# A causal depthwise convolution as matmuls: tap matrices stored channel by channel, and the preceding tokens copied by GpSimd

## The reference

```
def _causal_dwconv(x, w):
    k = w.shape[-1]
    xp = jnp.pad(x, ((0, 0), (k - 1, 0), (0, 0))).transpose(0, 2, 1)
    y = jax.lax.conv_general_dilated(xp, w[:, None, :], (1,), 'VALID', feature_group_count=w.shape[0], ...)
    return y.transpose(0, 2, 1)
...
local_short = fir(vh, fir_short_w)      # 5 taps a channel
local_long = fir(vh, fir_long_w)        # 64 taps a channel
```

## Time and profile before

| | |
|---|---|
| time of three runs | 6015.63, 6020.67, 6024.58 us; median 6020.67 |
| the profiled execution | 6031.09 us, its span 6029.3 us |
| the convolution, first to last matmul of L1155 | about 2734 to 3043 us of the span |
| busy over the whole span | PE 5421.1, PEld 4326.3, DVE 4262.5, ACT 2668.0, POOL 2549.7 us |
| mean granted clock of TensorE | 0.926 of 2.4 GHz |

### The profile page before, as it was taken

The page is one execution under the profiler, slowest core; times in us unless marked ns, Lnnn a source line. Parts: engine busy times, 40 slices in busy tenths (PEclk is TensorE's granted clock), DMA queues, the critical chain, the costliest instruction groups (busy, mean ns, idle before and its releaser), DMA issues. The chain is left out here.

```text
span 6029.3 us, 119845 instructions
## 1 busy us (share of the span) xinstructions
PE 5421.1 (90%) x42776; PEld 4326.3 (72%) x42776; DVE 4262.5 (71%) x13841; ACT 2668.0 (44%) x6214; POOL 2549.7 (42%) x3716
## 2 busy tenths in 40 slices
PE   6999999999999999979966645999999999999987
PEld 5888888888888888859954433777777777777765
DVE  4777777777777777752127885888887888888861
ACT  2555555555555555531133321444444444444441
POOL 1222222222222222210057751666666666666660
PEclk9999999999999999989965555999999999999998
DMA  1011101101110110118855542222222222222211
GB/s 41 29 34 36 33 31 36 36 29 34 36 36 29 34 36 29 34 39 186 201 140 147 141 111 63 61 62 61 61 61 61 61 61 62 61 62 61 61 35 44
DMA packets 603925, 373.22 MB, mean 62 GB/s; under 512 B 336528, under 2 KB 589264, under 8 KB 603344
## 3 DMA queue, kind: packets, MB, share of 16 engines
q1 hardware_dynamic: 532880, 329.91, 19.9%
q10 hardware_dynamic: 65664, 16.78, 1.2%
q0 software_dynamic: 4800, 18.88, 1.0%
HBM read 212.59 MB, written 137.10 MB: 58 GB/s over the span
## 5 line engine op out<-in xcount | busy, mean ns | idle before, releaser
L526 POOL TENSOR_TENSOR a_shift<-a_mean_var,a_eps 128x2 f32<-128x2 f32 x256 | 71.3, 278 | 1833.5 <-DVE a_mean_var L736 1833.5
L2125 PE MATMUL c_bank<-c_xT,c_gate 128*128 128x512 f32 x1024 | 499.8, 611 | 1.9 <-ACT c_statsT L1878 1.9
L750 DVE SCALAR_TENSOR_TENSOR a_cv<-a_raw,a_taps,a_cv 128x256 f32<-128x256 f32 x1152 | 461.9, 479 | 19.5 <-ACT a_cv L628 10.0
L820 PE MATMUL a_bank<-a_w,a_hidden 128*128 128x256 f32 x2048 | 459.1, 382 | 0.9 <-ACT a_hidden L613 0.9
L918 PE MATMUL a_bank<-a_turned,a_w 128*128 128x256 f32 x2048 | 453.0, 379 | 1.1 <-ACT a_turned L574 1.1
L820 PEld LDWEIGHTS a_bank<-a_w,a_hidden 128*128 128x128 f32 x2048 | 383.8, 190 | 71.8 <-issue 20.6
L918 PEld LDWEIGHTS a_bank<-a_turned,a_w 128*128 128x128 f32 x2048 | 384.0, 190 | 51.2 <-ACT a_turned L574 1.6
L1775 POOL TENSOR_TENSOR c_expd<-c_e,c_logit 128x16 f32<-128x16 f32 x128 | 371.7, 2904 | 51.1 <-DVE c_logit L1961 38.7
L1761 POOL TENSOR_TENSOR c_stats<-c_l2sq,half 128x16 f32<-128x16 f32 x128 | 373.4, 2917 | 17.8 <-DVE c_l2sq L1950 17.8
L2129 PEld LDWEIGHTS c_bank<-c_statsT,c_gate_stats 128*128 128x128 f32 x2048 | 270.1, 192 | 123.8 <-issue 123.8
L1345 POOL TENSOR_TENSOR i_coef<-i_base,i_exponent 128x12 f32<-128x12 f32 x128 | 298.6, 2332 | 76.7 <-issue 53.5
(11 more groups left out here) (294 smaller groups left out, 14194.1 us busy)
## 6 DMA issues: line engine op xcount, KB each, us to landing
a_x<-in_x SPq DMA_DIRECT2D x64, 256.0 KB, 3.3
scratch_xb<-a_xb SPq DMA_DIRECT2D x64, 256.0 KB, 2.1
scratch_q<-a_qkv_rows SPq DMA_DIRECT2D x64, 256.0 KB, 2.2
scratch_k<-a_qkv_rows SPq DMA_DIRECT2D x64, 256.0 KB, 2.7
scratch_v<-a_qkv_rows SPq DMA_DIRECT2D x64, 256.0 KB, 3.0
b_window<-scratch_v SPq DMA_DIRECT2D x8, 2048.0 KB, 22.2
scratch_long<-b_out ACTq DMA_DIRECT2D x8, 2048.0 KB, 24.6
scratch_short<-b_out POOLq DMA_DIRECT2D x8, 2048.0 KB, 18.4
```

Source lines behind the costliest of these rows:

```text
L750: ins = dve.scalar_tensor_tensor(cv[s][:, n, c], raw[s][:, n, c, j:j + TOK], taps[:, n, c, j:j + 1], cv[s][:, n, c], ALU.mult, ALU.add)
L820: ins = pe.matmul(dst[:, t * D:(t + 1) * D], src[s][:, c, tile_cols(t)], weight[:, c], start=(c == 0), stop=(c == chunks - 1))
L2125: pe.matmul(dst[:].rearrange("p (h t) -> p h t", h=H), gate1[:, c, cols], xT[sl][:, c:c + 1].broadcast_to([P, H, P]), start=(c == 0), stop ...
```

## The change

1. `matrix` becomes `[P, CH, K2, HALF]`: the 128 columns of a channel's matrix lie next to each other. The copies that fill it write in another order, and the matmul reads `matrix[g % 2][:, c]`. The windows keep their layout.
2. SP issues only loads. The copy of the preceding 64 tokens is made by GpSimd: 8 `tensor_copy`, one a sequence, each of 15 blocks of 64 elements on 64 partitions. It waits for the load of its unit. On GpSimd's list the shifts of units 0 and 1 come first, and that of unit u + 2 behind the short store of unit u.
3. TensorE waits for GpSimd's semaphore, which counts one a unit, instead of for the transfer's.

```diff
-        matrix = [sb(f"matrix{g}", [P, K2, HALF, CH]) for g in range(2)]
+        matrix = [sb(f"matrix{g}", [P, CH, K2, HALF]) for g in range(2)]
...
                 sp.dma_start(window[h][HALF:P], v_v[g, h]).then_inc(v_in[h], 16)
-                sp.wait_ge(v_in[h], 16 * (g + 1))
-                now, prev = (window[h][rows].rearrange("p (b n) c -> p b n c", b=SEQS)
-                             for rows in (slice(HALF, P), slice(0, HALF)))
-                sp.dma_start(prev[:, :, 1:WINDOWS], now[:, :, 0:WINDOWS - 1]).then_inc(window_in[h], 16)
...
+            def shift(u):
+
+                g, h = UNITS[u]
+                now, prev = (window[h][rows].rearrange("p (b n) c -> p b n c", b=SEQS)
+                             for rows in (slice(HALF, P), slice(0, HALF)))
+                pool.wait_ge(v_in[h], 16 * (g + 1))
+                for b in range(SEQS):
+                    ins = pool.tensor_copy(prev[:, b, 1:WINDOWS], now[:, b, 0:WINDOWS - 1])
+                ins.then_inc(window_in[h], 1)
+
+            for u in range(PARTS):
+                shift(u)
             for u, (g, h) in enumerate(UNITS):
                 for e in ("act", "dve"):
                     pool.wait_ge(out_made[e], counted(e, "out", u))
                 pool.dma_start(out_v["short"][g, h], out_sb[h][HALF:P]).then_inc(stored["short"][h], 16)
+                if u + PARTS < len(UNITS):
+                    shift(u + PARTS)
...
-                    ins = copy(matrix[g % 2][:, :, m * COLUMNS:(m + 1) * COLUMNS],
-                               src[:].rearrange("p (i k c) -> p k i c", k=K2, c=CH))
+                    ins = copy(matrix[g % 2][:, :, :, m * COLUMNS:(m + 1) * COLUMNS],
+                               src[:].rearrange("p (i k c) -> p c k i", k=K2, c=CH))
...
-                        pe.wait_ge(window_in[h], 16 * (g + 1))
+                        pe.wait_ge(window_in[h], g + 1)
...
-                        taps_of = matrix[g % 2][:].rearrange("p k i c -> p (k i) c")[:, :, c]
+                        taps_of = matrix[g % 2][:, c].rearrange("p k i -> p (k i)")
```

## The result

The changed kernel takes 5955.99 us (median of 4 runs, 5953.28 to 5959.14) against 6019.91 us (4 runs, 6015.63 to 6024.58) for the kernel before: 63.9 us less, ratio 0.9889 with a 95% interval of 0.9877 to 0.9902. The forecast was 5959.

A forecast was written before the change was run, and what follows sets the result against it. TensorE was taken to bound the filter phase. Packed weights would save 60 us and the earlier start 2, 62 in all, taking the median from 6020.7 to 5959; the forecast's own range was 5945 to 5995, eight in ten 5930 to 6012.

The forecast's parts named there:

- What bounds the kernel: Filter phase: TensorE is busy 308.7 of 309.0 us, so removing a transfer inside the stretch is worth nothing by itself.
- Step 1: Convolution matmuls: packing only the weights takes an entry from 0.279 to 0.22 us, saving 60 us over 1024 entries.
- Rival A: Convolution matmuls: the moving operand's step is free, 0.111 us an entry, some 137 us saved, 5884; chance 0.13.
- rival B: Convolution matmuls: the moving operand alone sets the pace, 0.26 to 0.279 us, giving 5999 to 6018; chance 0.13.
- Step 2: Copies out of PSUM that fill the matrices: writing runs of four with a stepped PSUM read costs 0.
- Step 3: SP's queue: eight shift transfers with a median of 12.0 us go, helping only a load that nobody waits for.
- The fear that loads 0 and 1 share the queue: Start of filter phase: load 0 could land later by at most 10 us if load 1 shares the queue's engines.
- Step 4: Shift on GpSimd: eight copies of 1.19 us, 9.5 us a unit, hidden behind TensorE's work except the first.
- Rivals C and D: GpSimd's shift copies: C, two-input price, 5985, chance 0.07; D, slower until they bound, 3.5 us eats the gain, 0.04.
- The start, 2.3 us: First unit: TensorE would start at 2731.5 instead of 2733.8, because the first, exposed shift gets shorter.
- The slack of 3.9 us: Window reload plus shift, 31.7 us, against TensorE's 35.6 on the other unit and one making of matrices.
- The late short store: GpSimd's list: where no making lies between, the next unit's short store starts 3.5 us late, but hidden.

The follow-up runs named there:

- Experiment 2: Kernel before with only the shift moved from SP's transfer to GpSimd copies, matrices still strided: 6024.2 us, ratio 0.9996.
- experiments 5 and 6: Changed kernel with the moving operand (5932.29 us), or the weights beside a packed moving operand (5948.95 us), read at steps of 4 to 256 bytes, unit by unit.
- experiment 7: Changed kernel with windows packed too, repacked from raw buffers by VectorE and GpSimd, and one matrix buffer: 5919.02 us, ratio 0.9825 to the kernel before.
- experiments 1 and 3: Changed kernel's packed matrices with the shift still a transfer, on SP's queue (5986.58 us, ratio 0.9938) or on GpSimd's queue (5992.79 us, 0.9944).
- Experiment 4: Changed kernel with each GpSimd shift copy made once more into a spare buffer: 5985.37 us, ratio 0.9935 to the kernel before.
- experiment 8: Kernel of experiment 7 with VectorE's repacking copies moved to ScalarE, GpSimd's kept: 5937.02 us, ratio 0.985 to the kernel before.

## Why the prediction was right, point by point

- **What bounds the kernel** (TensorE, until load, shift and matmuls become longer): right. Experiment 2 removes the transfer with TensorE unchanged, and the time does not move (0.9996).
- **Step 1, packed weights, 1024 x 0.059 = 60 us:** right, 61.0 of busy time. The pace of 0.22 was taken from four entries around the end of a bank and a pair of weight loads; the trace of the kernel before repeats them in every bank (ends 0.286 to 0.289 us apart, and 0.221 at the bank's last), and experiments 5 and 6 show 0.22 for each operand alone. That the rest up to 0.279 is both streams getting in each other's way fits all of this, but how they do it no run shows. Rival A (the moving step is free) and rival B (the moving operand alone costs 0.26 to 0.279) fall by the table: 220 ns. A was half right about what lies beyond: with both packed the pace is 112 ns, but the windows must be repacked, and experiment 7 gives 5919 and not 5884.
- **Step 2, the making of the matrices costs nothing:** right; L1090 takes 691 ns at the median where L1079 took 692, and a making 7.42 us, as before.
- **Step 3, the transfer off SP's queue helps only a load that nobody waits for:** true with the old matmul, not with the new one. The prediction priced the edit beside GpSimd's copies and never asked what the kernel would be with packed matrices and the transfer left in. By its own figures that would have been hidden (22.2 + 12.0 = 34.2 under 35.6), but the load no longer lands in 22.2: two units now offer 16.9 MB in less time, a load that meets the other window's shift takes 28.6 to 30.2 (experiments 1 and 3), and 24 to 30 us are lost. It did not spoil the sum, since both edits come together.
- **The fear that loads 0 and 1 share the queue:** not borne out. Load 0 landed 12.8 us after its issue.
- **Step 4, 1.19 us a copy and hidden:** mis-sized on the safe side, 0.94 (7.51 / 8), and 7.5 us a unit instead of 9.5. The Trainium skill, "GPSIMD Engine Reference", section "3.1 Elementwise — side-by-side cycle accounting", has a rate that gives an estimate of 0.82 us; the runs measure 0.94, between that and the 1.19 taken from affine_select. Rivals C and D needed 2.4 and 3.5 us a copy. Experiment 4, with 15.8 us a unit, shows that the chain they rest on is real.
- **The start, 2.3 us:** mis-sized; it was 3.8, from the shorter copies.
- **The slack of 3.9 us:** holds where a making of matrices lies between two uses of a window, at units 2 to 6. At the last unit it does not: 21.8 (load) + 7.5 stand against 28.2. 1.5 us were lost there that no step held, and at the 9.5 us assumed it would have been 3.5. The slack was worked out for one boundary and taken for all. It is luck that this miss and that of the start have the same size and cancel.
- **The late short store:** right in kind, far smaller. Where GpSimd is idle, the store starts 1.0 to 1.2 us after TensorE ends the unit (2760.76 after 2759.76), since the last banks must be copied first. Behind GpSimd's copies it is 1.9 us for unit (1,0) (2825.36 after 2823.45) and 1.2 for unit (3,0) (2952.00 after 2950.82). So a store is at most 0.9 us late and not 3.5, and no engine waited for it.
- **The range's upper end:** 5995 does not follow from its own terms. A pace of 0.25 saves 30 and a shared first load costs 8, which gives 5999. Nothing hangs on it here.

The sum, 62, came out as 61.0 + 3.8 - 1.5 = 63.3, against 63.9 between the medians.

## What to carry to other kernels

A matmul that reads either operand with a step of 16 bytes or more runs at half its pace here, whichever operand it is; packing one of two strided operands gives 0.28 to 0.22, packing the second 0.22 to 0.11, if the repacking finds an engine to do it. Work out the slack of a copy or transfer at each boundary, the last one above all, and again with the transfers' own time lengthened, because a faster engine asks for the same bytes in less time. An edit that is worth nothing alone can be worth over a third of the gain beside another: here 24 to 30 of 64 us.

## What the runs showed of the hardware

- A matmul strided by 256 bytes does not feel TensorE's lower clock. The changed kernel has 11 entries in 2 us at a granted clock of 0.50 (1.2 GHz) and 66 in 14 us at 0.99 (2.4 GHz). Entries overlap, so short stretches count more of them; their starts are 217 ns apart in the first and 220 in the second. L1166 alone, columns of the earlier trace rows:

```profile
2732.00:2734.00 2.00, 2.00 (x11) 2.00 (x11) 0.50 0.21 36
2736.00:2750.00 14.00, 14.00 (x66) 13.18 (x65) 0.99 0.01 1
```

  A packed one does: experiment 7 has 11 entries in 2 us at 0.50 and 92 in 10 us at 1.00, with starts 213 and 112 ns apart. So at 0.50 the strided and the packed pace are nearly equal, 217 and 213 ns.

```profile
2744.00:2746.00 2.00, 2.00 (x11) 2.00 (x11) 0.50 0.38 89
...
2850.00:2860.00 10.00, 10.00 (x92) 10.00 (x92) 1.00 1.10 282
```

- The worst steps are not the largest. 16 and 32 bytes cost 227 to 238 ns, 64 to 256 bytes 218 to 220, each step seen in one unit of one execution. No run here says why.
- Copies by VectorE and GpSimd from SBUF to SBUF that write with a step slow each other, 1.02 to 1.75 and 1.78 to 2.70 us, while ScalarE's (1.95 us) leave GpSimd's at 1.85. The kernel's plain copies out of PSUM by VectorE, 0.69 us, show no such change, nor do GpSimd's packed ones beside them (979 to 1018 ns in all 64). The two engines nearly take turns: alone 1.02 + 1.78 = 2.80 us, and side by side each starts a copy every 2.6 at the median. The Trainium skill, "SBUF — State Buffer", section "Who interferes with whom", describes a port pair that VectorE and GpSimd share, which whoever issues first holds for a whole instruction, for a VectorE copy with one SBUF input only in its two-port modes; the order of these numbers agrees, but no row names the mode of these copies. ScalarE, which that section of the Trainium skill keeps apart, left GpSimd alone.
- GpSimd copies between partition halves at no extra cost. In experiment 8 the first four copies of a unit read the other half of the partitions and the last four their own half: 1778 to 1785 ns against 1798 to 1802 in the first unit.
